# Matmul start flags in place of products of zeros that clear PSUM banks, in a graph network kernel on one Trainium2 core

## What is computed

```python
# layer 0: neighbour sums of h, and attention scores from signed masks
node_support = node_adj_norm @ h
hp = (node_adj > 0).astype(hW.dtype) @ hW
hm = (node_adj < 0).astype(hW.dtype) @ hW
e_plus = leaky_relu(concatenate([hp, hm], axis=1) @ a, ALPHA)[:, 0]
...
# layer 3
h = (x @ W).reshape(n, HEADS, C)                      # HEADS 4, C 64
e = leaky_relu(s_src[:, None, :] + s_dst[None, :, :], NEG_SLOPE)
e = where((adj > 0.5)[:, :, None], e, MASK_VAL)
alpha = softmax(e, axis=0)
out = einsum('ijh,ihc->jhc', alpha, h).reshape(n, HEADS * C) + bias
```

## Time and profile before

| | |
|---|---|
| three runs | 2115.57, 2115.84, 2117.70 us |
| the profiled execution, its own time | 2117.71 us |
| its span, first to last instruction | 2116.0 us |
| TensorE busy (matmul) | 2046.6 us, 97% |
| VectorE busy | 1526.1 us, 72% |
| ScalarE busy | 970.4 us, 46% |
| mean granted clock of TensorE | 0.991 of full |

### The profile page before, as it was taken

The page is one execution under the profiler, slowest core; times in us unless marked ns, Lnnn a source line. Parts: engine busy times, 40 slices in busy tenths (PEclk is TensorE's granted clock), DMA queues, the critical chain, the costliest instruction groups (busy, mean ns, idle before and its releaser), DMA issues.

```text
span 2116.0 us, 28365 instructions
## 1 busy us (share of the span) xinstructions
PE 2046.6 (97%) x10838; PEld 1156.1 (55%) x10847; DVE 1526.1 (72%) x2511; ACT 970.4 (46%) x1517; POOL 89.7 (4%) x113
## 2 busy tenths in 40 slices
PE   7999998799999998999999999999999999999997
PEld 4555665344444454555555544455899985333343
DVE  4665556798988877544578894344589987999988
ACT  3222224698988878755222220000411326654555
POOL 0000000000000000000000010000000102000000
PEclk9999999899999999999999999999999999999999
DMA  7665654355564554654000015444100004333331
GB/s 237 210 210 190 199 182 178 143 205 191 179 227 168 198 184 144 224 172 135 20 0 1 0 35 135 131 127 110 54 1 2 1 1 182 115 87 110 84 88 56
DMA packets 124647, 260.14 MB, mean 123 GB/s; under 512 B 14643, under 2 KB 54121, under 8 KB 121929
## 3 DMA queue, kind: packets, MB, share of 16 engines
q1 hardware_dynamic: 106185, 228.95, 34.0%
q10 hardware_dynamic: 18324, 29.34, 3.7%
HBM read 217.66 MB, written 40.59 MB: 122 GB/s over the span
## 4 chain that ended last, share of the span: by engine, by line
PE 72%; DVE 17%; ACT 6%; issue 2%; DMA 1%; POOL 0%; SPq 0%; DVEq 0%; ACTq 0%
PE banks L1083 21%; PE banks L1136 10%; PE banks L1170 9%; PE banks L986 9%; PE banks L1215 8%; PE banks L1234 4%; PE banks L975 3%; DVE arena L2300 3%; DVE arena L1832 2%; ACT arena L1361 2%; PE banks L889 2%; PE banks L1027 2%; DVE arena L1913 1%; DVE arena L2016 1%; DVE arena L2017 1%
## 5 line engine op out<-in xcount | busy, mean ns | idle before, releaser
L1083 PE MATMUL banks<-arena 128*128 128x512 f32 (+2 forms) x1512 | 583.2, 544 | 17.3 <-DVE arena L1913 17.2
L1083 PEld LDWEIGHTS banks<-arena 128*128 128x128 f32 x1512 | 282.8, 190 | 308.3 <-issue 229.1
L1913 DVE TENSOR_TENSOR arena<-arena 128x1536 f32<-128x1536 f32 (+4 forms) x132 | 201.9, 1529 | 150.2 <-ACT arena L1397 134.3
L2300 DVE SCALAR_TENSOR_TENSOR arena<-arena 128x1024 f32<-128x1024 f32 (+3 forms) x264 | 288.3, 1165 | 10.2 <-PE banks L1234 9.2
L1170 PE MATMUL banks<-arena 128*128 128x129 f32 (+1 forms) x1936 | 221.2, 276 | 3.5 <-DVE arena L2199 3.1
L986 PE MATMUL banks<-arena 128*128 128x512 f32 (+4 forms) x528 | 223.8, 545 | 0.2 <-ACT arena L1302 0.2
L1170 PEld LDWEIGHTS banks<-arena 128*128 128x128 f32 (+1 forms) x1936 | 217.8, 192 | 7.1 <-DVE arena L2199 3.8
L1215 PE MATMUL banks<-arena 128*32 128x512 f32 (+1 forms) x2112 | 215.5, 545 | 3.0 <-DVE arena L2300 3.0
L1136 PE MATMUL banks<-arena 128*128 128x512 f32 (+4 forms) x528 | 206.0, 544 | 1.2 <-DVE arena L2008 1.2
L1832 DVE CUSTOM_DVE_ANT_0 arena<-arena 128x2708 f32<-128x2708 bf16 (+1 forms) x66 | 196.2, 2973 | 2.2 <-DMA arena<-e_rows 1.9
L1397 ACT ACTIVATE arena<-arena 128x1536 f32<-128x1536 f32 (+4 forms) x132 | 170.6, 1292 | 57.3 <-DVE arena L1895 57.0
(11 more groups left out here) (245 smaller groups left out, 2197.1 us busy)
## 6 DMA issues: line engine op xcount, KB each, us to landing
arena<-hw_rows SPq DMA_DIRECT2D x126, 384.0 KB, 3.1
arena<-adj_T SPq DMA_DIRECT2D x126, 256.0 KB, 3.3
arena<-in_adj SPq DMA_DIRECT2D x17, 1354.0 KB
arena<-in_adj SPq DMA_DIRECT2D x42, 512.0 KB
adj_T<-arena ACTq DMA_DIRECT2D x63, 256.0 KB, 2.2
arena<-adj_T SPq DMA_DIRECT2D x84, 192.0 KB, 2.9
arena<-in_adj SPq DMA_DIRECT2D x15, 1024.0 KB
arena<-in_adj SPq DMA_DIRECT2D x15, 768.0 KB
```

Source lines behind the costliest of these rows:

```text
L1083: ins = PE.matmul(bank(2 * (c % 2) + f)[:, 0:wid(c)], hs[0:R, m % 3, h * D + f * P:h * D + (f + 1) * P], weights_of(n)[0:R, h, 0:wid(c)], ...
L1913: V.tensor_tensor(e, e, a, ALU.mult).then_inc(s["p_ok"], 1)
L2300: V.scalar_tensor_tensor(PM3[0:k, n % 3, h, 0:w], r3_bc[0:k, h, c * WW:c * WW + w], smalls[0:k, 4, h * T + t:h * T + t + 1], mask3[0:k, n ...
```

## The change

Every `opened` call goes, with the function, the tile `zrow` and GpSimd's memset of it. In sweep A the first narrow product of a chunk (t = 0, positive mask, first tile) carries the start flag; the others go on without it. In layer 3 each of the products at t = 0 carries it, so every 32-partition quarter of a bank is cleared by its own first product.

```diff
-        zrow = sb(BANK, dt=BF16)
...
-            G.memset(zrow, 0.0)
...
-        def opened(b):
-
-            PE.matmul(bank(b), zrow[:, 0:P], zrow, start=True, stop=True)
-
...
                 if t == 0:
                     if c >= 2:
                         pe.wait_ge(s["e21_free"], c - 1)
-                    opened(be)
                 pe.wait_ge(s["mask_ok"], n + 1)
...
                                         m[0:k, n % 2, r * R:(r + 1) * R], ub[0:k, t, :, lo:lo + wide_u],
-                                        start=False, stop=t == T - 1, skip_group_check=True)
+                                        start=t == 0 and m is Mp and r == 0, stop=t == T - 1, skip_group_check=True)
...
                     if c:
                         pe.wait_ge(l3_read, RAW3 * (c - 1) + h // 2 + 1)
-                    for v, w in halves(c):
-                        opened(h + v)
...
-                                        PM3[0:rows3(t), n % 3, h + q * DQ // C3, v * BANK:v * BANK + w], start=False, stop=t == T - 1,
+                                        PM3[0:rows3(t), n % 3, h + q * DQ // C3, v * BANK:v * BANK + w], start=t == 0, stop=t == T - 1,
                                         skip_group_check=True)
...
-                    for v, w in halves(c):
-                        opened(4 + v)
...
-                                        PM3[0:rows3(t), n % 3, h, v * BANK:v * BANK + w], start=False, stop=t == T - 1, skip_group_check=True)
+                                        PM3[0:rows3(t), n % 3, h, v * BANK:v * BANK + w], start=t == 0, stop=t == T - 1, skip_group_check=True)
```

## The result

The kernel after takes 2112.08 us (median of 9 runs, 2107.19 to 2114.50) against 2116.84 us for the kernel before on the same chips (9 runs, 2112.17 to 2121.17). The ratio is 0.9975, with a 95% interval of 0.9967 to 0.9984; 0.25% is 5.3 us, and 5.2 was the forecast. The interval reaches from 3.4 to 7.0 us, and the two medians lie 4.8 apart, so that the total agrees to 0.1 us is luck; the parts have to be seen in the trace. The forecast time, 2110.6, stood on the median of three runs; nine runs put that median 1.0 us higher. So the two profiles cannot be compared by their spans; they have to be compared place by place.

The account below looks back on a forecast made before the run. TensorE, busy 97% of the span and on 72% of the chain, was taken as the bound; 1.15 + 2.02 + 2.02 = 5.2 us off the three-run median 2115.84 gave 2110.6, range 2108.5 to 2113.0.

Parts of the forecast that it names:

- Sweep A, chunk 0: At sweep A's first chunk the zeros ran within TensorE's 0.9 us wait for VectorE's mask; removing them gains 0.
- Sweep A, chunks 1 to 5: At five later chunk starts of sweep A, each product of zeros costs 0.23 us on the chain; 1.15 us together.
- Layer 3, chunk 0: In layer 3's first chunk VectorE's weights bound the first units, so removing three pairs of zeros gains 0; other end 2.0.
- whatever TensorE gains: In layer 3's first chunk, all TensorE saves in unit 0 it stands still for by unit 3; net 0.
- Layer 3, chunks 1 and 2: First units of layer 3's later two chunks shorten 2.02 us each, 0.67 per pair including array mode changes; together 4.04.
- The gain passes: In layer 3's later chunks VectorE has slack and transposed degrees come first, so the chain behind moves by the whole gain.
- the second wait: VectorE's 0.98 us wait for the transposed degrees in layer 3's chunk 2, predicted to remain after the change.
- Edits at nothing: Dropping GpSimd's 0.53 us memset, moving later tiles' addresses and flagging products were each to cost or gain nothing.
- Streaming time only: In layer 3 only the zeros' streaming returns, 2.8 us; total gain 3.9, time 2111.9; chance 0.12.
- A costly flag: Flagged quarter products in sweep A and layer 3 each cost a pass, 12.2 us in all; time 2122.8; chance 0.03.
- A quarter's flag that clears the whole bank: A quarter's start flag wipes neighbouring quarters' results, spoiling sums but leaving the time as forecast; no chance of its own.
- Stretches at half clock: Clock falls at chunk ends, 1.7 us each: one more gives 2112.3, chance 0.13; one fewer 2108.9, chance 0.05.

Follow-up runs that it names:

- zeros in quarters: Kernel before, but each layer 3 bank cleared by four quarter products of zeros side by side instead of one full-width product; 2114.74 us, one execution.

## Why the prediction was right

- **Sweep A, chunk 0: 0.** No kernel leaves this one product out alone, but the traces settle it: from the first f32 load to the first narrow load it takes 2.92 us before and 2.93 after, and the matmul stream waits for VectorE's mask as long as before, 0.9 us.
- **Sweep A, chunks 1 to 5: 1.15 us.** Measured 0.22 us each, 1.1 us; the whole sweep is 1.08 us shorter where no stretch at half clock falls in.
- **Layer 3, chunk 0: 0.** Measured 0.2 us, so "whatever TensorE gains" was a little too strong. The step that VectorE bounds the first units held, and the run with GpSimd put off shows why VectorE is slow there, which the prediction took from a row without a cause. TensorE had only just caught up at unit 3: with the zeros doubled, unit 4 came 0.94 us later.
- **Layer 3, chunks 1 and 2: 2.02 us each.** Measured 2.02 and 2.03. The choice of 0.67 us per pair over 0.46 was right, and zeros in quarters show the reason that it gave: 0.44 without the change of width. By streaming time alone the sum would have been 3.9 us, 1.3 short of the forecast. The isolated gap of the Trainium skill's page "TensorE: Matmul & The Clock Gate" ("Back-to-back issue gap") prices the streaming share well: 216 ns, against 210 to 220 here. Its page "TensorEngine Tiling (Array Packing)" ("Key Properties") says that a change of tiling mode drains the engine; the trace agrees, with 0.23 us per pair.
- **The gain passes.** In the kernel after VectorE's idle time ahead of unit 25 has gone from 2.31 to 0.28 us, so what was slack there has been used up almost exactly. In chunk 2 the 1.99 us of waiting are gone, and the second wait still has 0.97 of its 0.98. The degrees still came later than VectorE's weights, and the end moved with them: from layer 3's first load to the end of the span it takes 333.8 us before and 329.6 after, all 4.2 us of the three chunks.
- **Edits at nothing** (flag, address, memset): borne out.
- **The rivals.** Streaming time only: fallen. A costly flag: fallen. A quarter's flag that clears the whole bank: fallen, since the kernel after still gives the right sums. They show as well that in sweep A the one flag on a product of 18 columns clears the bank for all 84 that are summed in it. Stretches at half clock: their price was right, 1.6 to 1.7 us each at a chunk start. They are more frequent than the prediction allowed for: totals of one kernel scatter over 6 to 10 us, and single profiles differ by twice the effect.

The sum in the traces is 1.1 + 0.2 + 4.05 = 5.3 us; the runs gave 0.9975 and 0.9978, 5.3 and 4.7 us.

## What to carry to other kernels

Cost a small operation on the busy engine by the distance between its neighbours in the chain, with and without it, and not by its duration or its count: here a product of zeros lasts 379 ns by its row, advances the stream by 215, and costs 335 where it breaks up quarter products. Then ask at each place who would have been next: of 24 such products 17 were on the path, and the other seven gave 0.2 us together. Where the total scatters by more than the effect, compare unit lengths; they repeated to 0.02 us while totals moved by 6 to 10.

## What was not expected of the hardware

The granted clock fell in the middle of sweep A while TensorE was busy throughout, always within a microsecond of the narrow products of the 20-row unit: six falls at the 21 starts of chunks 1 to 3 in the seven executions with zeros there, each 1.6 to 1.7 us, and none at the starts of chunks 4 and 5. Why it falls at some of these starts and not at others is open. And GpSimd's f32 and bf16 work on 128x256 slowed VectorE's scalar_tensor_tensor from 1284 ns to 1414 to 1709, although GpSimd works on other tiles than VectorE's weights read and write.
